# State-space stage of a one-core kernel: half of the products with B given to GpSimd

## The reference, cut to what matters

```
delta = softplus(dt_proj(dt_lo) + dt_proj_b)          # (b, e, t)
A     = -exp(A_log)                                   # (e, n)
def step(state, xs):                                  # over t = 0..511
    d_t, B_t, C_t, u_t = xs
    dA    = exp(d_t[..., None] * A)
    state = state * dA + (d_t * u_t)[..., None] * B_t[:, None, :]
    y_t   = einsum('ben,bn->be', state, C_t)
    return state, y_t
y = ys + D[None, :, None] * u
y = y * silu(z)
```

## Time and profile before

| | |
|---|---|
| median of 3 runs | 4474.57 us (4468.83 to 4490.4) |
| span of the profiled execution | 4489.8 us |
| time of that execution, as far as the runs show it (the highest of the three) | 4490.4 us |
| attention stage | 0 to about 2966 us |
| state-space rows, first `times_b` to last `times_c` | 2971.3 to 3682.2 us |
| VectorE busy over the whole span | 3306.1 us (74%) |
| GpSimd busy over the whole span | 956.6 us (21%) |

### The profile page before, as it was taken

How to read it: one execution, slowest core, us unless ns; L and a number is a source line. 1 busy time by engine, 2 the same in 40 slices (tenths; PEclk the granted TensorE clock), 3 DMA queues, 4 the chain that set the end, 5 groups by cost and what they waited for, 6 DMA issues and landing times. The chain is left out here.

```text
span 4489.8 us, 180202 instructions
## 1 busy us (share of the span) xinstructions
PE 4143.9 (92%) x76786; PEld 2588.5 (58%) x76786; DVE 3306.1 (74%) x5648; ACT 2301.9 (51%) x5547; POOL 956.6 (21%) x1800
## 2 busy tenths in 40 slices
PE   8999999999999999999999999758788768999999
PEld 4666667676766667666766667623333334444443
DVE  4888888888888888888888888649999981122221
ACT  4566666666666666666666666444444331111110
POOL 1333232333333232333333332200000000000000
PEclk8999999999999999999999999878988888999999
DMA  2212122221212122212212121132333323000000
GB/s 73 67 53 68 58 68 58 65 63 58 72 49 75 56 65 61 67 56 65 66 56 73 48 74 55 51 118 76 84 100 85 84 66 151 0 29 28 0 19 10
DMA packets 133581, 277.34 MB, mean 62 GB/s; under 512 B 20860, under 2 KB 62352, under 8 KB 129328
## 3 DMA queue, kind: packets, MB, share of 16 engines
q1 hardware_dynamic: 132640, 265.61, 19.4%
q10 hardware_dynamic: 144, 0.20, 0.0%
HBM read 235.09 MB, written 30.67 MB: 59 GB/s over the span
## 5 line engine op out<-in xcount | busy, mean ns | idle before, releaser
L414 PE MATMUL a_pb<-a_x_t,a_w_qkv 128*128 128x512 f32 x1536 | 839.0, 638 | 14.8 <-DMA a_x_t<-in_x_t 7.4
L1278 DVE TENSOR_TENSOR a_nq<-a_nq,a_tot 128x512 f32<-128x512 f32 x768 | 509.6, 705 | 131.4 <-PE a_pb L436 90.5
L1254 DVE SCALAR_TENSOR_TENSOR a_acc<-a_pb,a_taps,a_acc 128x511 f32<-128x511 f32 (+2 forms) x576 | 425.2, 738 | 43.5 <-ACT a_acc L847 13.8
L1974 PE MATMUL m_p_y<-m_h,m_ident 128*128 128x512 f32 x512 | 285.6, 710 | 120.5 <-DVE m_h L2172 120.5
L436 PEld LDWEIGHTS a_pb<-a_nq,a_ks 128*32 128x32 f32 x20480 | 213.4, 111 | 188.0 <-issue 108.4
L2440 PE MATMUL f_pb<-f_x_t,f_w_gu 128*128 128x512 f32 x704 | 308.0, 592 | 0.0
L414 PEld LDWEIGHTS a_pb<-a_x_t,a_w_qkv 128*128 128x128 f32 x1536 | 240.0, 191 | 99.4 <-issue 68.6
L1646 POOL COPY a_apt<-a_apt_fine 32x256 f32<-32x256 f32 x256 | 101.1, 395 | 913.0 <-DVE a_apt_fine L1299 887.5
L2494 ACT ACTIVATE f_gate<-f_pb 128x512 f32<-128x512 f32 x132 | 78.8, 597 | 411.7 <-PE f_pb L2440 275.3
L2166 DVE TENSOR_TENSOR_SCAN m_h<-m_da,m_h 128x2048 f32<-128x2048 f32 x64 | 283.1, 4424 | 6.8 <-ACT m_da L2095 1.4
L436 PE MATMUL a_pb<-a_nq,a_ks 128*32 128x32 f32 x20480 | 251.3, 200 | 29.5 <-DVE a_nq L1415 15.6
(11 more groups left out here) (295 smaller groups left out, 9095.1 us busy)
## 6 DMA issues: line engine op xcount, KB each, us to landing
a_rows<-rows SPq DMA_DIRECT2D x192, 512.0 KB, 3.8
a_amp_sums<-amp_sums SPq DMA_DIRECT2D x64, 508.0 KB, 3.7
attn_o<-a_o_t SPq DMA_DIRECT2D x64, 256.0 KB, 2.5
m_b_rows<-ssm_bc SPq DMA_DIRECT2D x64, 256.0 KB, 3.6
m_c_rows<-ssm_bc SPq DMA_DIRECT2D x64, 256.0 KB, 4.6
m_o_t<-attn_o SPq DMA_DIRECT2D x16, 1024.0 KB, 8.7
a_w_qkv<-in_w_qkv SPq DMA_DIRECT2D x48, 256.0 KB, 2.8
f_w_gu<-in_w_gu SPq DMA_DIRECT2D x3, 1536.0 KB, 17.1
```

The costliest lines, as they stand in the source:

```text
L414: mm = nc.tensor.matmul(pb[:, V_BANK if i == P_V else KQ_BANK], w_qkv[:, i, k], x_t[:, k, b * T:(b + 1) * T], start=(k == 0), stop=(k == D ...
L1254: last = nc.vector.scalar_tensor_tensor(acc[:, i, d:T], src[:, 0:T - d], taps[:, i, 3 - d:4 - d], acc[:, i, d:T], ALU.mult, ALU.add)
L1278: last = nc.vector.tensor_tensor(part, part, spread(blocks, shape), ALU.mult)
L1974: nc.tensor.matmul(p_y[:, et], ident[:], h[:, (b * DS + n) % 3, et], start=(n == 0), stop=(n == DS - 1), skip_group_check=True).then_inc(s ...
```

## The change

`times_b` is split. VectorE makes the product for the lower two channel tiles (128 x 1024 elements), and GpSimd, in a stream of its own that runs through all 64 rows, makes that for the upper two. GpSimd waits for the same things as VectorE did: the row of B, `du`, and `summed` of row - 3. A new semaphore `upper_ready` counts its products. `scan` waits for it as well, and so does ScalarE where it reuses the buffer of `du`.

```diff
+        LOWER, UPPER = slice(0, ET // 2), slice(ET // 2, ET)
...
                                 act.wait_ge(dbu_ready, (b - 1) * DS)
+                                act.wait_ge(upper_ready, (b - 1) * DS)
...
-                    nc.vector.tensor_tensor(h[:, row % 3], du[:, b % 2], spread(b_rows[:, row % ROWS:row % ROWS + 1], [P, ET, T]),
+                    nc.vector.tensor_tensor(h[:, row % 3, LOWER], du[:, b % 2, LOWER],
+                                            spread(b_rows[:, row % ROWS:row % ROWS + 1], [P, ET // 2, T]),
                                             ALU.mult).then_inc(dbu_ready, 1)
...
                 def scan(row):
                     dve.wait_ge(da_ready, (row + 1) * ET)
                     dve.wait_ge(dbu_ready, row + 1)
+                    dve.wait_ge(upper_ready, row + 1)
...
+            @block.gpsimd
+            def _(pool):
+                for row in range(B * DS):
+                    b, n = divmod(row, DS)
+                    pool.wait_ge(b_in[row % ROWS], 16 * (row // ROWS + 1))
+                    if n == 0:
+                        pool.wait_ge(du_ready, b + 1)
+                    if row >= 3:
+                        pool.wait_ge(summed, (row - 2) * ET)
+                    nc.gpsimd.tensor_tensor(h[:, row % 3, UPPER], du[:, b % 2, UPPER],
+                                            spread(b_rows[:, row % ROWS:row % ROWS + 1], [P, ET // 2, T]),
+                                            ALU.mult).then_inc(upper_ready, 1)
```

More of the change, by code:

```diff
@@ L1800, in ssm_block_stage @@
         dbu_ready = sem("dbu_ready")
+        upper_ready = sem("upper_ready")
         scanned = sem("scanned")
```

## The result

The changed kernel takes 4512.04 us in the median of 4 runs (4505.72 to 4524.32), the kernel before 4473.78 (4468.83 to 4490.4, 4 runs). The ratio is 1.0083, with a 95% interval of 1.0060 to 1.0105: slower by 27 to 47 us, 38 us by the medians. Forecast were 4508 us and +34 us.

The account below looks back on a forecast made before the run. VectorE was taken to bound the state-space rows. 61 rows x (2.10 - 1.07) = +63 us, -21 hidden, -14 shrinking waits, +6 scan waits gave +34 on 4474.6: 4508 us, 8-in-10 range 4462 to 4556.

Parts of the forecast that it names:

- Exclusion, read from the attention stage: GpSimd copies there suggested that VectorE instructions with two SBUF inputs and GpSimd exclude each other, each waiting a whole instruction.
- The first rival: State-space rows: scan and GpSimd don't exclude one another, so GpSimd's product hides in the scan; 4424 us, chance 0.16.
- GpSimd's price, 2.1 us: Time that GpSimd's product of 1024 elements takes from VectorE, taken as the middle of 1.55 and 2.6 us.
- the lower bound: GpSimd's product at 1.55 us, from its copies in attention with the two inputs read in turn.
- The upper bound: GpSimd's product at 2.6 us, from its products of 4 and 8 elements, 2.5 ns an element.
- The third rival: State-space rows: GpSimd's product is cheap, 1.55 us; +7 us, 4482 us, chance 0.12.
- The saving, 65 us: VectorE's halved `times_b` falls from 2.286 to 1.22 us, 1.07 us in each of 61 rows, if GpSimd's half cost nothing.
- When GpSimd's half runs: GpSimd mostly becomes ready within the scan and goes in ahead of `times_c`, which waits 2.1 us; a row takes 10.0 us.
- The sign "`times_c` with a median near 4.3 us": Expected in the changed kernel's profile: VectorE's product with C at a median near 4.3 us, with a minimum of 2.27.
- Hidden, and waits that shrink: GpSimd's time behind scans beside PSUM or one-input instructions, -21 us; shorter waits for the projection, -12, and sums, -2.
- The scan's waits for GpSimd: Where GpSimd comes last, the scan waits for its fixed part and semaphore: 20 rows of 0.3 us, +6 us.
- The base: The +34 us was added to the median 4474.6 us, as the profiled execution, 4490.4, lies 16 us above it.

Follow-up runs that it names:

- the last version: Against the kernel before: GpSimd makes the upper half in 18 chosen rows only, VectorE's taps and finish moved behind scans; 4472.37 us against 4479.72, ratio 0.9988.

## Why the prediction was right, step by step

- **Exclusion, read from the attention stage.** Right, for the scan too: two scans of the changed kernel were lengthened (to 6.47 us), and GpSimd's products stood through scans. The first rival falls with that. What the prediction did not have: GpSimd does not always get in at the next boundary between two instructions of VectorE. Twice it let a scan pass first; why stays open.
- **GpSimd's price, 2.1 us.** Measured 4.38 - 2.27 = 2.11. The value was the middle of bounds that lay 1 us apart, so this closeness is luck; at the lower bound the sum would have been +7, hardly a loss. The upper bound, 2.5 ns an element, was read off 10 ns between the least of one line and the median of another, for 4 and 8 elements; the sizes of the experiments give 2.0 to 2.1. The 2.25 us named beside it was worked out from a figure for an add of 2048 elements, not for a product; the product of 1024 takes 2.34 when it is alone. The third rival falls by the same 2.11.
- **The saving, 65 us.** Right: 1.219 us for the half product, and 38 to 59 us of gain with GpSimd out of the way.
- **When GpSimd's half runs.** Half right. The means of the groups give the lengthening: 64 x 0.99 us on the product with C (63 us), 63 x 0.475 on the product with B (30 us), 64 x 0.063 on the scan (4 us). I had it all ahead of the product with C. For 14 of the 64 rows the sums or the row of B came after the scan's end, and GpSimd took its turn one instruction later. The price is nearly the same there (3375 - 1219 = 2.16 us in the median), so the sum didn't suffer. The sign "`times_c` with a median near 4.3 us" failed: 33 of the 64 are lengthened, and the median is 2.83.
- **Hidden, and waits that shrink.** The lengthening is 97 us, 93 of it behind the first tap, against 61 x 2.11 = 129: 36 us were not paid, where I had 21 for hidden and about 6 for GpSimd's part in the waits for the projection. On the other side the wait for the projection shrank by 6.5 us (16.6 to 10.1), as much as the longer rows were to take from it. But that for the sums rose from 4.5 to 9.5 (forecast -2). The scan's waits for GpSimd came to 7 us behind the first tap, near the forecast 6, and that is luck: the forecast had 20 rows of 0.3, the run has three waits of 2.35, in row 11 of three sequences. The forecast comes to -65 + 101 - 2 = +34, where 101 is the lengthening (61 x 2.10 - 21 - 6) and -2 the idle time; the run has -65 + 93.2 + 3.5 = +31.7. So two errors of 8 and 6 us nearly cancel, and the total is closer than its terms.
- **The base.** Adding the sum to the median and not to the profiled execution was right. The profiled execution of the kernel before lies 16 us above the median, and its first tap comes 16.3 us later than in the changed kernel's, which has nothing to do with the change. That the slow 16 us lie there is read from one execution of each.

## What to carry to other kernels

Before giving elementwise work to GpSimd, look at what VectorE does at that time. Beside instructions with two SBUF inputs GpSimd added nothing here, and its two-input product took from VectorE twice what it saved. What it could do without lengthening anything was a product beside VectorE's instructions that read PSUM or have one input (15 in the last version) or in a wait of VectorE's (3), and a memset, which only writes. Even then longer waits took 7 of 19 us back. To find this out ahead, look among the lines of the engine that should be relieved for one whose maximum lies above its median by a fixed amount, as 886 above 691 ns, and see what GpSimd does at that moment.

## What the runs showed of the hardware that had not been expected

- Beside VectorE's product with C, GpSimd's two-input product costs 2.0 to 2.06 ns an element (2.11 us for 1024, 1.63 for 800, 1.02 for 512, medians of the lengthened products), its copy 0.77 (0.79 us for 1024). That is 2.7 times, not twice, the price of one input.
- An instruction of GpSimd that only writes is not touched by VectorE's two-input instructions, nor they by it: 64 memsets with 952 to 955 ns, 38 of them wholly within such an instruction.
- A product that was ready early went ahead of a scan and lengthened it from 4.42 to 5.97 us. So a placing can be spoilt by the other engine being early.
- Who goes first is not settled by waiting alone: of GpSimd's 63 products that stood behind VectorE, 61 went in at the end of the instruction that they met, and two let one more scan pass (7.91 us for 2.34). No run tells why.
